# A decoder's selective scan as one block: one half of the tokens behind the other, B and C split into bf16 parts per half, outputs added up in token-major form, and the norm merged into the block

## What is computed

```
def _L1_attn_ref(x, W_dt, b_dt, W_B, W_C, D_param, A_log, gamma, beta):
    Bsz, L, D, N = (2, 256, 128, 16)
    ...
    xn = (x - mu) * jax.lax.rsqrt(var + LN_EPS) * gamma + beta
    dt = jax.nn.softplus(xn @ W_dt.T + b_dt)
    A = -jnp.exp(A_log)
    B_in = xn @ W_B.T
    C_in = xn @ W_C.T
    A_bar = jnp.exp(dt[..., None] * A)
    Bx = dt[..., None] * B_in[:, :, None, :] * xn[..., None]
    def step(h, inputs):
        a_t, bx_t, c_t = inputs
        h = a_t * h + bx_t
        y_t = jnp.einsum('bn,bdn->bd', c_t, h)
        return (h, y_t)
    ...
    y = jnp.transpose(ys, (1, 0, 2)) + D_param * residual
```

## Time and profile before

| | us |
|---|---|
| median of 3 runs | 1780.19 (1778.75 to 1781.52) |
| the profiled execution | 1779.27 |
| its span in the profile | 1777.5 |
| mean granted clock of PE, as a share of full speed | 0.899 |
| PE, DVE, ACT, POOL busy | 1499.6, 1063.5, 646.7, 217.7 |
| first instruction of the scan stage to its last | 400.34 to 505.46 |

### The profile page before, as it was taken

The page is one execution under the profiler, slowest core; times in us unless marked ns, Lnnn a source line. Parts: engine busy times, 40 slices in busy tenths (PEclk is TensorE's granted clock), DMA queues, the critical chain, the costliest instruction groups (busy, mean ns, idle before and its releaser), DMA issues. The chain is left out here.

```text
span 1777.5 us, 22019 instructions
## 1 busy us (share of the span) xinstructions
PE 1499.6 (84%) x8172; PEld 686.7 (39%) x8172; DVE 1063.5 (60%) x2616; ACT 646.7 (36%) x936; POOL 217.7 (12%) x231
## 2 busy tenths in 40 slices
PE   2997889985777999998979998988988589996985
PEld 2232344431233344445433333354436323344353
DVE  6796454458946777754454972556455647755354
ACT  3465432224325033333424663422221245552431
POOL 3000010000000533331000000000000103331000
PEclk9898789998969999998987998998996679997788
DMA  5000000020000100000020000000010000000000
GB/s 207 1 1 1 1 1 0 1 104 35 1 0 1 48 1 1 1 1 1 1 78 26 1 1 1 1 1 1 0 72 1 1 1 1 1 1 1 1 1 12
DMA packets 4075, 27.16 MB, mean 15 GB/s; under 512 B 384, under 2 KB 2432, under 8 KB 2944
## 3 DMA queue, kind: packets, MB, share of 16 engines
q1 hardware_dynamic: 2912, 25.22, 3.6%
q10 hardware_dynamic: 1056, 0.52, 0.1%
HBM read 25.21 MB, written 0.52 MB: 14 GB/s over the span
## 5 line engine op out<-in xcount | busy, mean ns | idle before, releaser
L811 DVE TENSOR_REDUCE maxima<-banks 128x1 f32<-128x512 f32 (+4 forms) x640 | 363.1, 604 | 111.0 <-PE banks L660 104.3
L955 ACT ACTIVATE big<-banks 128x1024 f32<-128x1024 f32 (+2 forms) x320 | 294.3, 960 | 265.5 <-PE banks L703 94.2
L688 PE MATMUL banks<-big 32*128 32x512 f32 (+6 forms) x1280 | 232.6, 613 | 17.2 <-DVE big L832 12.9
L660 PE MATMUL banks<-big 32*128 32x77 bf16 (+6 forms) x1024 | 158.3, 297 | 23.5 <-ACT big L238 6.1
L1476 DVE TENSOR_TENSOR big<-big,banks 128x512 f32<-128x512 f32 (+1 forms) x116 | 79.7, 687 | 152.6 <-PE banks L1389 147.2
L724 PE MATMUL banks<-big,v_heads 128*9 128x512 f32 (+7 forms) x1024 | 159.6, 569 | 6.3 <-ACT heads_out L871 3.2
L477 POOL TENSOR_TENSOR rstd<-mean_var,minus_half 128x4 f32<-128x4 f32 x34 | 34.9, 1026 | 1033.9 <-DVE mean_var L399 1033.9
L1451 ACT ACTIVATE big<-banks 128x512 f32<-128x512 f32 (+1 forms) x116 | 69.1, 596 | 179.1 <-PE banks L1388 179.0
L660 PEld LDWEIGHTS banks<-big 32*128 32x128 bf16 (+1 forms) x1024 | 57.3, 97 | 182.0 <-DVE maxima L811 93.5
L1419 PE MATMUL banks<-big,moe_weights 128*128 128x512 f32 (+1 forms) x232 | 119.8, 601 | 3.0 <-ACT big L1459 2.6
L688 PEld LDWEIGHTS banks<-big 32*128 32x128 f32 (+3 forms) x1280 | 72.8, 178 | 70.3 <-ACT big L955 23.7
(11 more groups left out here) (410 smaller groups left out, 2216.5 us busy)
## 6 DMA issues: line engine op xcount, KB each, us to landing
moe_weights<-in_moe SPq DMA_DIRECT2D x1, 4864.0 KB, 14.5
moe_weights<-in_moe SPq DMA_DIRECT2D x1, 4768.0 KB, 22.5
moe_weights<-in_moe SPq DMA_DIRECT2D x1, 3264.0 KB, 10.5
moe_weights<-in_l3x SPq DMA_DIRECT2D x1, 3072.0 KB, 9.6
late_weights<-in_l2x SPq DMA_DIRECT2D x1, 2048.0 KB, 8.8
moe_weights<-in_l SPq DMA_DIRECT2D x1, 1234.0 KB, 13.1
rows<-in_rows SPq DMA_DIRECT2D x1, 1152.0 KB, 8.1
late_weights<-in_turned SPq DMA_DIRECT2D x1, 1152.0 KB, 16.9
```

The source lines that it names most:

```text
L660: last = nc.tensor.matmul(RING[n % NR][:, x * klen:x * klen + last_key(t)], q[rows, t * P:(t + 1) * P], ks[rows, 0:last_key(t)], start=Tru ...
L688: last = nc.tensor.matmul(SC[pair % 2][0:size, j % 2, n0:S], ks[rows, i * P:i * P + size], q[rows, n0:S], start=True, stop=turned)
L811: nc.vector.tensor_reduce(dst, src, AX_X, ALU.max).then_inc(ring_free.up(), 1)
L955: nc.scalar.activation(E[pair % NEP][0:size, :, n0:S], SC[pair % 2][0:size, :, n0:S], ACT.Exp, scale=scale).then_inc(exp_ready.up(), 1)
```

## The change

The four blocks become one, and the order of work in it is written out by hand:

- The softplus is taken apart by halves. DVE reads the product directly from PSUM with the bias added (two TENSOR_SCALARs and a subtraction, L1742 to L1745 of the new file), ACT's Exp and Ln are done per half, and `time_steps(z)` (dt, u) comes before the loop for half 0, but behind step 2 of the loop for half 1.
- B and C of half 0 are split in bf16 parts by DVE as before. Those of half 1 are split on ACT and PE between steps of the loop: ACT copies the product from bank 7 to bf16, PE subtracts that copy from the bank (`take_part_off`, a bf16 matmul with minus the identity), ACT copies what is left, twice (behind steps 2, 5 and 8 on ACT; behind steps 4 and 7 on PE).
- All of `pick` is written by one POOL copy of 96x4096.
- The loop does half 0 completely and then half 1: `steps = [(n, z) for z in range(2) for n in range(N)]`.
- Outputs are added up turned: `ch` in four 128x128 tiles is the stationary operand and the identity the moving one (`tile_products`), so that banks 6 and 7 collect token-major sums. D times the residual is added in the same banks by four float32 matmuls per half with the diagonal matrix `diag`. L1703 and the turning back (L335) go away.
- The norm's work for half 0 stands inside the loop of half 1: sum and statistics behind step 17, norming behind step 19 (DVE), turning in PE behind step 21, one copy on ACT behind step 23.

```diff
@@ Norms @@
+    def turn_half(self, pe, half):
+        c = self.c
+        pe.wait_ge(self.norm_ready.sem, self.norm_ready.at(2 * half + 2))
+        for k, t in enumerate(self.tiles(half)):
+            last = c.nc.tensor.transpose(c.bank[self.TURNED[2 * half]][:, k * P:(k + 1) * P], self.final.out[:, t, :], c.ident[:])
+        last.then_inc(self.turned_ready.up(2), 2)
...
@@ layer1_scan @@
+    own = Norms(c, None, [Norm(c.X, turned=[(c.XT, None, None)])], c.X, sums=(6, 7), turned=(6, None, 0, 1))
+    zs = [slice(z * S, (z + 1) * S) for z in range(2)]
+    steps = [(n, z) for z in range(2) for n in range(N)]
+    LAST = len(steps) - 1
+    def tile_products(z, src, right, start, stop):
+        for k in range(ST):
+            last = nc.tensor.matmul(c.bank[own.SUM[z]][:, k * P:(k + 1) * P], src[:, k * P:(k + 1) * P], right, start=start and k == 0,
+                                    stop=stop and k == ST - 1, skip_group_check=True)
+        return last
     with nc.Block() as block:
         @block.tensor
         def _(pe):
             def inputs(s):
                 n, z = steps[s]
                 if s >= 3:
                     pe.wait_ge(ch_ready.sem, ch_ready.at(s - 2))
+                for j in range(2):
+                    last = nc.tensor.matmul(c.bank[2 * (s % 3) + j][:, :], pick[:, j * N + n, :], bc[:, zs[z]], start=True, stop=True)
+                last.then_inc(in_ready.up(), 1)
+            def take_part_off(i):
+                pe.wait_ge(bc_act.sem, bc_act.at(i))
+                nc.tensor.matmul(c.bank[7][0:96, :], minus_id, bc[:, zs[1]], start=False, stop=True, skip_group_check=True).then_inc(
+                    part_off.up(), 1)
+            for z in range(2):
+                nc.tensor.matmul(c.bank[z][:, :], c.m("L1_WdtT"), xnT[:, zs[z]], start=True, stop=True).then_inc(dt_made.up(), 1)
+            pe.wait_ge(weights_ready.sem, weights_ready.at(1))
+            for z in range(2):
+                nc.tensor.matmul(c.bank[(2, 7)[z]][0:96, :], weights.rearrange("p k n -> p (k n)"), xnT[:, zs[z]], start=True, stop=True).then_inc(bc_made.up(), 1)
+            pe.wait_ge(diag_ready.sem, diag_ready.at(1))
+            tile_products(0, c.XT[:, zs[0]], diag, True, False)
+            pe.wait_ge(dt_read.sem, dt_read.at(2))
+            pe.wait_ge(pick_made.sem, pick_made.at(1))
+            pe.wait_ge(bc_dve.sem, bc_dve.at(1))
             inputs(0)
             inputs(1)
             for s, (n, z) in enumerate(steps):
+                if s < LAST - 1:
                     inputs(s + 2)
                 pe.wait_ge(ch_ready.sem, ch_ready.at(s + 1))
+                done = own.sum_ready if n == N - 1 else summed
+                tile_products(z, ch[:, s % 2, :], c.ident[:], False, n == N - 1).then_inc(done.up(), 1)
+                if s in (4, 7):
+                    take_part_off((s - 1) // 3)
+                if s == 10:
+                    pe.wait_ge(bc_act.sem, bc_act.at(3))
+                    tile_products(1, c.XT[:, zs[1]], diag, True, False)
+                if s == 21:
+                    own.turn_half(pe, 0)
+            own.turn_pair(pe, 2)
+            own.turn_pair(pe, 3)
         @block.scalar
         def _(act):
+            scalar.activation(c.negA, c.m("L1_A_log"), ACT.Exp).then_inc(neg_ready.up(), 1)
+            for z in range(2):
+                act.wait_ge(abs_ready.sem, abs_ready.at(z + 1))
+                last = scalar.activation(ex[:, zs[z]], ex[:, zs[z]], ACT.Exp)
+            seq(act, act_step, last)
+            for z in range(2):
+                scalar.activation(ex[:, zs[z]], ex[:, zs[z]], ACT.Ln, bias=1.0).then_inc(soft_ready.up(), 1)
             for s, (n, z) in enumerate(steps):
+                if n == 0:
+                    act.wait_ge(dt_ready.sem, dt_ready.at(z + 1))
                 if s >= 2:
                     act.wait_ge(decay_used.sem, decay_used.at(s - 1))
+                scalar.activation(a[:, s % 2, :], dtT[:, zs[z]], ACT.Exp, scale=c.negA[:, n:n + 1]).then_inc(a_ready.up(), 1)
+                if s == 2:
+                    act.wait_ge(bc_made.sem, bc_made.at(2))
+                    scalar.copy(bc[:, zs[1]], c.bank[7][0:96, :]).then_inc(bc_act.up(), 1)
+                if s == 5:
+                    act.wait_ge(part_off.sem, part_off.at(1))
+                    scalar.copy(bc[32:64, zs[1]], c.bank[7][32:64, :])
+                    scalar.copy(bc[64:96, zs[1]], c.bank[7][64:96, :]).then_inc(bc_act.up(), 1)
+                if s == 8:
+                    act.wait_ge(part_off.sem, part_off.at(2))
+                    scalar.copy(bc[64:96, zs[1]], c.bank[7][64:96, :]).then_inc(bc_act.up(), 1)
+                if s == 23:
+                    own.move_half(act, scalar, 0)
+            own.move_pair(act, scalar, 2)
         @block.vector
         def _(dve):
             def drive(s):
                 _, z = steps[s]
                 dve.wait_ge(in_ready.sem, in_ready.at(s + 1))
+                vector.tensor_tensor(bx[:, s % 2, :], uT[:, zs[z]], c.bank[2 * (s % 3)][:, :], ALU.mult).then_inc(driven.up(), 1)
+            def time_steps(z):
+                dve.wait_ge(soft_ready.sem, soft_ready.at(z + 1))
+                seq(dve, step, vector.tensor_tensor(dtT[:, zs[z]], mx[:, zs[z]], ex[:, zs[z]], ALU.add))
+                if z == 0:
+                    dve.wait_ge(neg_ready.sem, neg_ready.at(1))
+                    vector.tensor_scalar(c.negA, c.negA, -1.0, None, ALU.mult)
+                seq(dve, step, vector.tensor_tensor(uT[:, zs[z]], dtT[:, zs[z]], xnT[:, zs[z]], ALU.mult))
+                vector.tensor_copy(c.small[:, z:z + 1], dtT[:, z * S:z * S + 1]).then_inc(dt_ready.up(), 1)
+            vector.tensor_scalar(minus_id, c.ident_bf[0:96, 0:96], -1.0, None, ALU.mult)
+            vector.tensor_scalar(diag, c.ident[:], c.col("L1_attn_D_param"), None, ALU.mult).then_inc(diag_ready.up(), 1)
+            for z in range(2):
+                dve.wait_ge(dt_made.sem, dt_made.at(z + 1))
+                vector.tensor_scalar(ex[:, zs[z]], c.bank[z][:, :], c.col("L1_attn_b_dt"), 0.0, ALU.add, ALU.min)
+                vector.tensor_scalar(mx[:, zs[z]], c.bank[z][:, :], c.col("L1_attn_b_dt"), 0.0, ALU.add, ALU.max).then_inc(dt_read.up(), 1)
+                dve.wait_ge(dt_read.sem, dt_read.at(z + 1))
+                vector.tensor_tensor(ex[:, zs[z]], ex[:, zs[z]], mx[:, zs[z]], ALU.subtract).then_inc(abs_ready.up(), 1)
+            dve.wait_ge(bc_made.sem, bc_made.at(1))
+            seq(dve, step, vector.tensor_copy(bc[:, zs[0]], c.bank[2][0:96, :]))
+            seq(dve, step, vector.tensor_tensor(rest, c.bank[2][0:96, :], bc[:, zs[0]], ALU.subtract))
+            vector.tensor_copy(bc[32:64, zs[0]], rest[32:64, :])
+            seq(dve, step, vector.tensor_copy(mid[64:96, zs[0]], rest[64:96, :]))
+            vector.tensor_tensor(bc[64:96, zs[0]], rest[64:96, :], mid[64:96, zs[0]], ALU.subtract).then_inc(bc_dve.up(), 1)
+            time_steps(0)
             drive(0)
+            for s, (n, z) in enumerate(steps):
                 dve.wait_ge(driven.sem, driven.at(s + 1))
                 dve.wait_ge(a_ready.sem, a_ready.at(s + 1))
+                vector.tensor_tensor_scan(h[:, s % 2, :], a[:, s % 2, :], bx[:, s % 2, :], 0.0, ALU.mult, ALU.add).then_inc(decay_used.up(), 1)
+                if s < LAST:
                     drive(s + 1)
                 dve.wait_ge(decay_used.sem, decay_used.at(s + 1))
+                if s - 2 == N - 1:
+                    dve.wait_ge(own.sum_ready.sem, own.sum_ready.at(1))
+                elif s >= 2:
+                    dve.wait_ge(summed.sem, summed.at(s - 1 - (s - 2) // N))
+                vector.tensor_tensor(ch[:, s % 2, :], h[:, s % 2, :], c.bank[2 * (s % 3) + 1][:, :], ALU.mult).then_inc(ch_ready.up(), 1)
+                if s == 2:
+                    time_steps(1)
+                if s == 17:
+                    own.own_sum(dve, 0)
+                    own.own_stats(dve, 0, 0)
+                if s == 19:
+                    own.own_norm(dve, 0, 0)
+            own.own_sum(dve, 1)
+            own.own_stats(dve, 0, 1)
+            own.own_norm(dve, 0, 1)
+            own.move_pair(dve, vector, 3)
+        @block.gpsimd
+        def _(pool):
+            nc.gpsimd.tensor_copy(weights[:, :, 0:N], c.m("L1_WBT").unsqueeze(1).broadcast_to([P, 3, N]))
+            nc.gpsimd.tensor_copy(weights[:, :, N:2 * N], c.m("L1_WCT").unsqueeze(1).broadcast_to([P, 3, N])).then_inc(weights_ready.up(), 1)
+            nc.gpsimd.tensor_copy(pick, c.pick_id[:].unsqueeze(2).broadcast_to([96, 2 * N, P])).then_inc(pick_made.up(), 1)
+            own.power(pool, 0, 0)
+            own.power(pool, 0, 1)
```

139 lines of the change are left out of this document (47 added, 92 removed).

## The result

The changed kernel takes 1773.41 us, the median of 22 runs, against 1780.01 us for the kernel before, measured beside it 22 times. The ratio is 0.9968, with a 95% interval of 0.9959 to 0.9976: 4.3 to 7.3 us faster, 5.7 in the middle. The forecast was 1774.0 us.

What follows compares the result with a forecast made beforehand. DVE, full in the loop, was taken as the bound, so gains lie outside it. Terms -7.5 + 4.7 + 1.7 - 5.1 = -6.2 us take the profiled 1779.27 to 1773.1, median 1774.0; range 1768.0 to 1778.0.

Steps and rivals of the forecast that it cites:

- What bounds the stage: In the loop DVE is always busy and alone sets the 2.31 us step; a change can only win outside it.
- term C: In the loop, decays queued behind ACT's copies delay scans 6 and 9 by 1.1 and 0.6 us: +1.7 us.
- Term A: At the stage's start, the new order brings the first scan from 419.99 to 412.5, despite a POOL hold-up: -7.5 us.
- Term B: In the loop, half 1's dt and u and half 0's norm put work on DVE, which counts in full: +4.7 us.
- Rival 2: Lower clock still holds at steps 4 and 7, or the start gains only 7.0 us: 1776.5 to 1777; chance 0.16.
- Term D: At the stage's end, PE's last tiles to the last copy take 6.8 us against 11.84: -5.1 us.
- PE and its loads: In each loop step, PE's eight weight loads are nearly all hidden; if none were, the sum is 2.6 us worse.
- Rival 1: Clock survives the stage's end, so the next stage's 13 us on PE take about 6.5: 1767.5 us; chance 0.14.
- The signs of being wrong: Gaps behind PE in the loop, half clock beyond step 7, or a changed length of the next stage's first 22 us.

Runs made afterwards that it cites:

- e7: Changed kernel with half 1's bf16 parts made by DVE behind step 2, without ACT's copies and PE's subtractions; median 1776.2 us, ratio 0.9984.
- e2: Changed kernel with half 0's norm (sum, statistics, norming) taken out of the loop and put behind it; median 1770.6 us, ratio 0.9952.
- e3_pick_act: Changed kernel with three quarters of `pick` written by ACT and a quarter by POOL; median 1776.0 us, ratio 0.9981.
- e4: Changed kernel with four unread float32 products added on PE behind the loop's last tiles; median 1770.8 us, ratio 0.9948.
- e6: The changed kernel run again unaltered; median 1774.5 us, ratio 0.9974; its profiled execution took 1779.94 us.
- e8: Changed kernel with five extra DVE rows, 3.6 us with their signals, ahead of the first drive; median 1779.5 us, ratio 0.9989.
- e9: Changed kernel with outputs added up feature-major again, each half turned back by PE, half 0's norm two steps later; median 1775.6 us, ratio 0.9983.

## Why the prediction was right

**What bounds the stage.** Shown: in the first profile DVE has no gap in the loop but the two of term C and the one ahead of the first scan, and the rows put into the loop (e7) or taken out of it (e2) changed it by their full length.

**Term A, -7.5.** Measured from the stage's first product 12.02 against 19.65, so -7.6. The subtraction ended 0.65 us sooner than forecast (404.50 instead of 405.15): half of that is the stage itself, which began 0.33 us earlier, the rest mostly the POOL copy, which ended at 403.95 instead of 404.5. It ended 0.55 us behind POOL's end, about its own 0.69. So the hold-up was worth 1.2 us, not 1.6. That the hold-up is POOL's is shown by e3_pick_act. The Trainium skill, "SBUF — State Buffer", on the shared port pair, has the later one wait for the whole of the other's instruction; these rows agree with 1.91 us against 0.69. No run undoes the other parts of the new start (the softplus by halves, the product read directly from PSUM), so how the -7.6 divides among them is not shown.

**Term B, +4.7.** Measured 1.53 (dt and u: 418.97 to 420.50), 2.13 and 1.02: 4.7. POOL's power beside scan(18) cost DVE nothing, as forecast: the scan began 0.17 us ahead of it and took its usual 1.22 us. What was held up is POOL's row, 1.85 us in place of the 1.01 at the end of the stage; it ended 0.80 us behind the scan, and the norming that needs it stands two steps later.

**Term C, +1.7, the term that was mis-sized: 2.9.** The first gap is 1.17 against 1.1, the second 1.71 against 0.6, since a dip of the clock fell on step 7. Rival 2 named this as a condition ("a dip at one of the two places") and priced it. In the six other profiles with this placement (e2, e3, e4, e6, e8, e9) the two gaps sum to 2.9 to 4.3: in every profile taken, half clock reached one or both places, so the condition of Rival 2, which had 0.16, is the rule, and the 0.6 for the second gap at full clock was never met. The mechanism and its prices hold: the first gap at full clock is 1.17 both times (here and in e8), and with half clock at both places, in e4 and e9, the two sum to 4.25 and 4.24, where the prediction's sum for that was 4.2. What failed is the premise that PE is at full clock at steps 4 and 7. It came from one rise of the clock in the old trace, which the prediction puts at 426.3; a mean of 0.93 over 426 to 430 puts it at 426.6.

**Term D, -5.1.** Measured 6.85 against 11.84, -5.0. e9_unturned shows 1.97 of it as the turned sum's; the rest, by the rows that are missing, is one half's norm, a barrier and the rows behind it, which no run took apart. But e2_tail shows that half 0's norm need not have gone into the loop for it.

**PE and its loads.** Four tiles take 1.16 us from first start to last end, one old product 1.12; the half-clock tiles 2.08, against 2.02 taken. In the Trainium skill's terms ("TensorE: Matmul & The Clock Gate", on LDWEIGHTS) eight loads of 0.107 us would have shown if none were hidden; they did not, and undoing them closed no gap.

**The sum.** -7.6 + 4.7 + 2.9 - 5.0 = -5.0, and the stage's -4.9 agrees. The forecast median, 1774.0, was met at 1773.4 although term C took 1.2 us more than said: the whole kernel gained 1.7 us more at the median than the stage did in the first profile, which no term of the sum holds. So that the median came within 0.6 us of the forecast is in part luck: one error was made up by another. Profiles tie such differences to half-clock stretches in other stages. The text gave these "1 to 2 us"; two profiles of one kernel differ by 8.9, 7.6 of it outside the stage. Rival 1 (the next stage at full clock) did not happen in its form; in the first profile its stretch was 10 us shorter, in e6_again it was not. What makes a stretch longer or shorter in a given execution stays open.

**The signs of being wrong.** Two of the three that the prediction names came in the first profile: half clock lasted from step 7's tiles into step 11 (433 to 443), and the next stage changed its length by 4.1 us. The third, a gap behind PE in the loop, came in e6_again with 0.63 us. What they say against is the account of the clock; the terms of the stage, measured one by one, stand but for C.
